# Layer 4 of a four-layer conditional network: the 48 units in another order

## The reference, cut to what matters

```python
rw = softmax(router_logits); w, sel = top_k(rw, 2); w = w / w.sum()
out = sum over e of dense_w[b, e] * mlp(x, gate[e], up[e], down[e])   # two experts for each batch
out = out + mlp(x, shared_gate, shared_up, shared_down)               # one for all batches
# mlp: (gelu(x @ gate) * (x @ up)) @ down, with 128 -> 512 -> 128
x = x + out
```

## Time and profile before

| | |
|---|---|
| time, median of 3 runs | 153.3 us (152.61 to 153.38) |
| profiled execution, own time | 152.91 us |
| its span | 151.0 us |
| PE busy | 146.4 us, 97% |
| DVE busy | 110.2 us, 73% |
| POOL busy | 93.0 us, 62% |
| ACT busy | 71.8 us, 48% |
| granted TensorE clock | 1.00 over the whole span |

### The profile page before, as it was taken

One profiled execution on the slowest core, in us unless ns is written; L12 is line 12 of the kernel. 1 busy time (PEld: TensorE's weight loads), 2 busy tenths in 40 slices (PEclk: granted clock), 3 DMA queues, 4 the chain that ended last, 5 costly groups with the idle time before them and its releaser, 6 DMA issues.

```text
span 151.0 us, 3154 instructions
## 1 busy us (share of the span) xinstructions
PE 146.4 (97%) x1091; PEld 133.7 (89%) x1091; DVE 110.2 (73%) x231; ACT 71.8 (48%) x140; POOL 93.0 (62%) x101
## 2 busy tenths in 40 slices
PE   7999999999999999999999999999999999999992
PEld 2478999999978999899989999999999999999891
DVE  3985666667996586777875968886587886868792
ACT  3775444460375554454454354545435334246560
POOL 1004999999900007849994939996875999890000
PEclk9999999999999999999999999999999999999999
DMA  3999999972544587293297486086448038000052
GB/s 69 424 401 397 415 403 397 417 291 78 235 183 137 147 167 250 65 300 126 65 332 224 153 256 226 9 260 247 187 96 301 24 106 308 10 0 0 4 208 69
DMA packets 13919, 30.15 MB, mean 200 GB/s; under 512 B 1344, under 2 KB 8016, under 8 KB 13776
## 3 DMA queue, kind: packets, MB, share of 16 engines
q1 hardware_dynamic: 13472, 28.76, 55.1%
q10 hardware_dynamic: 432, 1.19, 2.2%
HBM read 24.71 MB, written 1.05 MB: 171 GB/s over the span
## 4 chain that ended last, share of the span: by engine, by line
PE 88%; DVE 4%; POOL 3%; ACT 1%; issue 1%; POOLq 0%
PE pair L571 22%; PE pair L561 12%; PE acc L620 11%; PE pair L507 9%; PE pair L578 8%; PE acc L605 7%; PE acc L515 5%; PE acc L629 5%; PE acc L462 3%; PE pair L540 2%; PE pair L469 2%; POOL duo_lo L378 2%; DVE x_hl L760 2%; ACT mix_raw L402 1%; PE pair L547 1%; POOL duo_hi L375 1%
## 5 line engine op out<-in xcount | busy, mean ns | idle before, releaser
L378 POOL TENSOR_TENSOR duo_lo<-raw_duo,duo_hi 128x512 fp32r<-128x512 f32 x36 | 49.1, 1364 | 2.9
L787 DVE TENSOR_TENSOR hid_lo<-hid,hid_hi 128x512 fp32r<-128x512 f32 (+1 forms) x42 | 36.3, 865 | 17.1 <-ACT hid_hi L438 16.5
L438 ACT ACTIVATE hid_hi<-hid 128x512 fp32r<-128x512 f32 (+1 forms) x42 | 25.7, 612 | 43.4 <-DVE hid L794 40.2
L375 POOL CAST duo_hi<-raw_duo 128x512 fp32r<-128x512 f32 x36 | 28.4, 788 | 27.2 <-PE acc L620 27.2
L794 DVE TENSOR_TENSOR hid<-pair,act 128x512 f32<-128x512 f32 (+1 forms) x50 | 33.1, 663 | 5.6 <-PE pair L571 4.1
L571 PE MATMUL pair<-x_duo,duo_hi 128*128 128x256 f32 x192 | 35.1, 281 | 0.2 <-POOL duo_lo L378 0.2
L423 ACT ACTIVATE act<-pair 128x512 f32<-128x512 f32 x47 | 27.7, 589 | 9.6 <-PE pair L571 7.7
L571 PEld LDWEIGHTS pair<-x_duo,duo_hi 128*128 128x128 f32 x192 | 29.6, 188 | 0.8 <-issue 0.3
L571 PE MATMUL pair<-x_duo,duo_lo 128*128 128x256 f32 x96 | 26.8, 279 | 0.0
L561 PE MATMUL pair<-x_hl,shared_hi 128*128 128x512 f32 x64 | 20.5, 402 | 0.0
L571 PEld LDWEIGHTS pair<-x_duo,duo_lo 128*128 128x128 f32 x96 | 18.0, 188 | 0.0
(11 more groups left out here) (102 smaller groups left out, 200.3 us busy)
## 6 DMA issues: line engine op xcount, KB each, us to landing
raw_duo<-experts SPq DMA_DIRECT2D x12, 768.0 KB, 5.2
ring<-experts SPq DMA_DIRECT2D x16, 386.5 KB, 7.0
raw_solo<-experts SPq DMA_DIRECT2D x8, 768.0 KB, 4.9
x_duo<-x_hl SPq DMA_DIRECT2D x24, 128.0 KB, 3.7
x<-xT ACTq DMA_DIRECT2D x1, 1024.0 KB, 6.2
lora_raw<-x SPq DMA_DIRECT2D x4, 256.0 KB, 2.3
raw_solo<-shared SPq DMA_DIRECT2D x1, 768.0 KB, 9.8
out<-lora_raw SPq DMA_DIRECT2D x3, 256.0 KB, 2.7
```

The costliest lines, as they stand in the source:

```text
L375: pool.tensor_copy(duo_hi[:, j % HALVES, piece(n)], raw_duo[:, j % RAWS, piece(n)])\
L378: pool.tensor_tensor(duo_lo[:, j % HALVES, piece(n)], raw_duo[:, j % RAWS, piece(n)], duo_hi[:, j % HALVES, piece(n)].bitcast(F32), ALU.su ...
L438: act.activation(hid_hi[:, k % SPLITS, half(u, i)], hid3[:, u % PAIRS, half(u, i)], ACT.Copy)\
L787: dve.tensor_tensor(hid_lo[:, k % SPLITS, half(u, i)], hid3[:, u % PAIRS, half(u, i)], hid_hi[:, k % SPLITS, half(u, i)].bitcast(F32), ALU ...
```

## The change

```diff
-ORDER = _s[:4]
-for _n in range(3):
-    _di, _si, _ri = _d[6 * _n:6 * _n + 6], _s[3 * _n + 4:min(3 * _n + 7, 12)], _r[2 * _n:2 * _n + 2]
-    ORDER += _di[0:2] + _si[0:1] + _ri[0:1] + _di[2:4] + _si[1:2] + _di[4:6] + _ri[1:2] + _si[2:3]
-ORDER += _d[18:20] + _r[6:7] + _d[20:22] + _r[7:8] + _d[22:24] + _s[12:16]
+ORDER = _s[:2] + _r[:1] + _s[2:4]
+for _n in range(DUOS):
+    ORDER += _d[2 * _n:2 * _n + 2]
+    if _n % 3 != 2:
+        ORDER += _s[2 * (_n // 3) + _n % 3 + 4:][:1]
+    if _n % 3 != 1 and _n < DUOS - 1:
+        ORDER += _r[2 * (_n // 3) + _n % 3 // 2 + 1:][:1]
+ORDER += _s[12:16]
```

## The result

The changed kernel is slower: 154.46 us median of 4 runs (154.25 to 154.75) against 152.97 (152.61 to 153.38), a ratio of 1.0085, 95% interval 1.0055 to 1.0115. I had forecast no change, and the time lies above my range as well. The profiled execution has its own time at 154.57 and a span of 152.6, 1.6 above that of before.

The account below looks back on a forecast made before the run. PE sets the pace, so an order can win only what PE loses between units. Terms: -0.38 - 0.66 + 1.01 = -0.03 us, so 153.3 us, forecast range 152.8 to 153.8 (chance 0.74); 8 in 10: 152.3 to 153.9.

Parts of the forecast that it names:

- R0 third: Start of layer 4: 0.38 us of PE work moves into the 0.40 idle before the first down product; gain 0.38.
- The late stretch: D8 to D11: PE's losses of 0.41 at D9, 0.09 at D10.0 and 0.16 at R6 go; gain 0.66.
- The distance of five: Before D3.0, D6.0 and D9.0: PE waits for POOL's two pieces, 0.41, 0.30 and 0.30 us; cost 1.01.
- S2.3 at position 41: Late in layer 4: PE has 4.2 us of work against one DVE addition; costs nothing, and the tail moves along.
- the second rival: From D10.0 to S3.3, nine units with no R between: DVE falls behind, 0.9 us over, 154.2; chance 0.06.
- DVE's additions: Between an R unit and the couple beside it: PE losing time there would show the prediction wrong; no size given.

Follow-up runs that it names:

- the experiment: The changed order with the single unit R0 moved back from third to fifth place; layer 4 109.21 us, +0.43 against the changed order, ratio 1.0118 to the kernel before.
- the order before with light subtractions: Kernel before with POOL's subtraction for the couples cut from 512 to 32 columns a piece, their low part left out; layer 4 106.28 us, ratio 0.9942.
- light couples 10 and 11: Changed order with POOL's subtraction cut to 32 columns a piece for couples 10 and 11 alone; layer 4 107.98 us, -0.80 against the changed order.
- The order with the longest low parts: Same units reordered, R0 third, every couple six or more positions after the down product freeing its buffer, single before shared unit; ratios 0.9975 and 0.9980 to kernel before.

## Why the prediction was wrong

*What bounds the kernel.* Right: PE, and only its pauses count. The table of pauses accounts for 1.50 of the 1.54.

*R0 third, gain 0.38.* Right in size, 0.41 on the timeline and 0.43 by the experiment.

*The late stretch, gain 0.66.* By the chain's pieces 0.41 + 0.25; by the starts of matmuls 0.41 + 0.40. Mis-sized by 0.15, on the good side. That the 0.16 at R6 went is in part luck: I gave the distance as the reason, and it was a wait for an addition (below).

*The distance of five, cost 1.01.* The mechanism was right and all three places were named. I took 0.41 for D3.0 and 0.30 for the others; they measured 0.42, 0.39 and 0.41. The reason to shade them, that DVE would be ahead and shift its low parts, was wrong: the pieces of couples 3, 6 and 9 took the 4.48 of couples with the same neighbours. Mis-sized by 0.21.

*"S2.3 at position 41. ... It costs nothing. The last six units keep their order, so the tail and the stores move with the rest."* This is the step that failed most clearly. S2.3's own bank indeed costs nothing, but what counts is that R7 left position 41: a single spares DVE a low part and ACT a high part just before six units in which each step of DVE follows on ACT and back. Without it D11.0's low part is done 0.90 before PE needs it (139.84 to 140.74), in place of 1.98 before (137.45 to 139.43), and the last two down products wait 0.52. DVE and PE, first before, then after:

```profile
136.76 0.69 DVE L787 TENSOR_TENSOR hid_lo<-hid,hid_hi 128x512 fp32r<-128x512 f32 x1
139.43 0.28 PE L620 MATMUL acc<-hid_hi,duo_hi 128*128 128x256 f32 x1
```

```profile
139.15 0.69 DVE L790 TENSOR_TENSOR hid_lo<-hid,hid_hi 128x512 fp32r<-128x512 f32 x1 [0.17 <-ACT hid_hi L441]
140.74 0.28 PE L623 MATMUL acc<-hid_hi,duo_hi 128*128 128x256 f32 x1
```

The missing single and the blocked low parts are both needed for it: with R7 back at 41 the 0.52 is gone, and with light couples 10 and 11 as well. I had this as the second rival, at 0.9 us for 0.06: the mechanism was there and its chance was too small. Its price came from three low parts of 1.80; one of 1.68 and one of 1.04, D10.0's and D10.1's, were enough for the 0.52. That its 154.2 lies near the 154.46 that came out is luck, as the tail is 0.52 of the 2.72 us of costs below.

*No term for DVE's additions.* This is the largest of the terms left out. I named them at the end as what would make the prediction wrong, and gave them no price. In the order before, the singles that stand alone between couples, R5 to R7, already showed it: R6's down product, the 1.05 for 0.89, starts at 130.18, just after D9.1's addition ended at 129.42 + 0.61, and I booked it as a loss that goes. The lines, of DVE and PE:

```profile
129.42 0.61 DVE L811 SCALAR_TENSOR_TENSOR lora_raw<-acc,w_col,lora_raw 128x128 f32 x2
130.18 1.13 PE L629 MATMUL acc<-hid,raw_solo 128*128 128x128 f32 x8
```

This loss is not POOL's: the order before with light subtractions has it too, 0.16. In the new order R2, R4 and R6 stand so, and it cost 0.63 (0.19 of it before R2, which is not POOL's), with 0.21 more in small pauses and 0.14 for two more gate products behind a single.

So gains of 0.41 and 0.81 stood against costs of 1.22 + 0.63 + 0.21 + 0.14 + 0.52 = 2.72: +1.50. The failure is one of counting: I priced the change by the waits that the old trace named, and took every other edge between engines, which had just been met in the old order, as free in the new one.

The port rule of the Trainium skill ("SBUF — State Buffer", Who interferes with whom) holds in each trace here: each low part of layer 4 over 512 columns that starts while a piece of POOL runs ends 0.54 to 0.69 us after that piece, and the ones that start free take 0.68 to 0.70. But the length that it adds is not the price. The order with the longest low parts, 1.004 on average, has the shortest layer 4 of all kernels here with full subtractions (106.73, and 107.35 the second time, with the wait for the gather).

## What to carry to other kernels

In a schedule with PE at 97%, a new order must be priced at every edge where two engines meet, with the slack of each one at its new place; a wait that the old trace doesn't show may be only just met, and not absent. Give an engine that runs level with PE its light units late, before a stretch in which nothing lets it catch up. And measure a stage from its own start: the start of layer 4 moved by up to 1.1 us between executions, as much as most effects here.

## What was not expected of the hardware

After a pause PE's next piece is slow: at each wait for POOL the couple's twelve matmuls then take 1.48, from their first start to the next step's, in place of 1.40, and eight of a single's down product 0.88 in place of 0.81. And a gate product of shared or coupled units that follows a single's 128-column down product takes 1.47 in place of 1.40, in both orders. The granted clock was 1.00 in both executions; no run here shows the reason.
